# A two-layer conditional mixture-of-experts kernel on one core: LoRA sums, slot table and attention loop rearranged

## The reference, cut to what matters

```python
w = cond_weights[conditions]                     # layer 0: a 32x32 matrix for each batch
y = einsum('bct,bcd->bdt', x, w)
logits = y @ gate.T + 2 * y @ (gate_B @ gate_A).T
top 2 of 8 experts; gup = y @ gate_up + 2 * (y @ A.T) @ B.T   # LoRA of rank 16
out = silu(gates) * h @ down + 2 * LoRA          # 256 -> 128 -> 256
x = x + weighted sum of the two experts' rows
q, k, v = x @ Wq, Wk, Wv; rms norm, rope          # layer 1: 8 heads, 4 key groups, 32 wide
k_blocks[blk, :, off] = k; v_blocks[...] = v      # written over a cache of 4112 blocks of 16 rows
o = softmax(q k^T / 16, window of 128) v; o @ Wo
out = top 1 of 2 experts of width 1024, times its probability; x = x + out
```

## Time and profile before

| | |
|---|---|
| median of 3 runs | 1004.19 us (1002.6 to 1004.86) |
| profiled execution | 1012.61 us, span 1010.6 us, mean PE clock 0.905 |
| PE busy | 864.8 us, 86% of the span |
| DVE, POOL, ACT busy | 601.9, 432.6, 419.4 us |
| chain that ended last | PE 67%, DVE 13%, DMA 8%, issue 6% |
| HBM | 151.92 MB read, 41.75 MB written |

### The profile page before, as it was taken

The page is one execution under the profiler, slowest core; times in us unless marked ns, Lnnn a source line. Parts: engine busy times, 40 slices in busy tenths (PEclk is TensorE's granted clock), DMA queues, the critical chain, the costliest instruction groups (busy, mean ns, idle before and its releaser), DMA issues.

```text
span 1010.6 us, 28469 instructions
## 1 busy us (share of the span) xinstructions
PE 864.8 (86%) x9102; PEld 658.2 (65%) x9102; DVE 601.9 (60%) x2374; ACT 419.4 (42%) x1293; POOL 432.6 (43%) x454
## 2 busy tenths in 40 slices
PE   4778879999576766079999999999949999999996
PEld 2436758888332322047777777777739999999995
DVE  6518946777489999454778778787812222222221
ACT  2332113333143333043767767676713333333331
POOL 0105255554477772432455656556212233333332
PEclk9976789999799889555999999999968999999998
DMA  6973845556754441242455555555235565656561
GB/s 181 335 291 143 268 161 158 164 161 151 246 166 142 142 144 60 77 117 69 121 154 140 142 139 144 144 143 151 73 129 167 188 216 185 210 181 210 192 203 37
DMA packets 103850, 162.85 MB, mean 161 GB/s; under 512 B 29129, under 2 KB 83963, under 8 KB 98224
## 3 DMA queue, kind: packets, MB, share of 16 engines
q1 hardware_dynamic: 66768, 85.55, 26.3%
q0 software_dynamic: 32208, 68.36, 23.8%
q10 hardware_dynamic: 4800, 7.96, 2.5%
HBM read 151.92 MB, written 41.75 MB: 192 GB/s over the span
## 4 chain that ended last, share of the span: by engine, by line
PE 67%; DVE 13%; DMA 8%; issue 6%; POOL 2%; ACT 1%; DVEq 1%; SPq 0%; POOLq 0%; ACTq 0%
PE bank L958 12%; PE bank L969 11%; PE bank L930 8%; PE bank L942 7%; PE bank L831 6%; PE bank L910 6%; DMA work<-in_x 4%; PE bank L918 4%; PE bank L895 3%; PE bank L823 3%; DVE work L1162 2%; DVE work L1341 2%; POOL work L478 2%; DVE work L1338 2%; PE bank L839 2%
## 5 line engine op out<-in xcount | busy, mean ns | idle before, releaser
L1430 DVE TENSOR_TENSOR work<-bank,work 128x512 f32<-128x512 f32 x66 | 45.7, 692 | 166.9 <-ACT work L708 166.9
L958 PE MATMUL bank<-work,experts 128*128 128x128 f32 x1056 | 130.9, 278 | 0.5 <-ACT work L700 0.5
L958 PEld LDWEIGHTS bank<-work,experts 128*128 128x128 f32 x1056 | 127.9, 195 | 2.5 <-ACT work L700 0.9
L969 PE MATMUL bank<-experts,work 128*128 x528 | 124.6, 379 | 0.0
L691 ACT ACTIVATE work<-work 128x164 f32<-128x164 f32 x256 | 107.7, 425 | 22.1 <-DVE work L1418 21.9
L478 POOL DMA_INDIRECT kvring<-in_cache,read_i x64 | 65.2, 1018 | 100.8 <-PE bank L942 35.6
L677 ACT ACTIVATE wqkv_sb<-bank 105x512 f32<-105x512 f32 x128 | 75.8, 592 | 75.1 <-PE bank L930 74.2
L482 POOL DMA_INDIRECT out_x<-work x33 | 33.5, 1017 | 164.5 <-DVE work L1442 158.9
L969 PEld LDWEIGHTS bank<-experts,work 128*128 128x128 f32 x528 | 95.4, 190 | 10.3
L478 POOL DMA_INDIRECT work<-y_rows,index_work x72 | 67.8, 942 | 70.1 <-PE bank L839 46.8
L855 PE MATMUL bank<-wqkv_sb,work 128*128 128x512 f32 x128 | 73.4, 702 | 21.1 <-DVE work L1329 21.1
(11 more groups left out here) (244 smaller groups left out, 1596.9 us busy)
## 6 DMA issues: line engine op xcount, KB each, us to landing
experts<-in_fc SPq DMA_DIRECT2D x33, 1024.0 KB, 5.2
work<-cst SPq DMA_DIRECT2D x128, 82.0 KB
slots_out<-work SPq DMA_DIRECT2D x72, 128.0 KB, 2.3
work<-in_x SPq DMA_DIRECT2D x64, 128.0 KB, 3.1
written_blocks<-kvring POOLq DMA_DIRECT2D x3, 2048.0 KB, 7.6
slots_in<-fill ACTq DMA_DIRECT2D x1, 4257.0 KB, 21.9
work<-slots_in SPq DMA_DIRECT2D x33, 129.0 KB, 5.1
y_rows<-rows SPq DMA_DIRECT2D x8, 512.0 KB, 6.1
```

Source lines behind the costliest of these rows:

```text
L958: mm = pe.matmul(bank[1 + n][:, k * P:k * P + P], fc_s[tile % 2][:, h * H1 + n * 512 + k * P:h * H1 + n * 512 + k * P + P], yst[tile % 2][ ...
L969: mm = pe.matmul(bank[5 + tile % 2][:, 0:D], av[n][:, k * P:k * P + P], proj_v[:, (4 * n + k) * D:][:, bass.ds(expert, D)], start=(n == 0 ...
```

## The change

Stage 1: two of the four block-diagonal DMAs go from SP to ACT. The LoRA factors are loaded by eight DMAs of POOL at the start, even experts to partitions 0 to 15 and odd ones to 64 to 79. The expert weights are loaded in two halves by ACT at tiles 5 and 10. The LoRA products move from after the last tile into the loop over tiles (PE at steps 13 to 27, two experts side by side), and DVE adds them to the weights. The block copies start after 26 tiles. `match_blocks` and `owners` move into stage 2 as index steps 3 to 23, all later index steps move back by 10 or 20. `hi_hot` becomes one DVE instruction for a chunk, and ACT multiplies by the token's number in eight. The slot buffer is filled by 17 DMAs in stage 2.

Stage 3 and 4: the ring has 12 places (four in the room of the gate-up weights), and its first 12 `cached` gathers are started within stage 3, one for every second tile from tile 4. The attention goes by couples: at each step PE does the first batch's values of couple s-3, the key transposes of couple s+2, the ranks at every fourth step, both batches' transposed probabilities of couple s-2 (two PSUM banks), the output product at every second step, the second batch's values of couple s-3 and both batches' scores of couple s+1 (one pair of banks for a couple).

```diff
-RING = 8
+RING = 12
@@ sync, scalar: block-diagonal DMAs
-            for j in range(BT):
+            for j in range(2):
                 sp.dma_start(bd[...], cw_dram...).then_inc(s1_bd, 16)
+            for j in range(2, BT):
+                act.dma_start(bd[...], cw_dram...).then_inc(s1_bd, 16)
@@ gpsimd, stage 1
+            for j in range(2):
+                place = lora[64 * j:64 * j + R0, :].rearrange("r (k c) -> r k c", c=896)
+                for a, c0, width in ((gup_a, 0, 256), (gup_bt, 256, 256), (down_a, 512, 128), (down_bt, 640, 256)):
+                    pool.dma_start(place[:, :, c0:c0 + width], ...).then_inc(s_lora, 16)
-            pool.wait_ge(s1_yc, 12)
+            pool.wait_ge(s1_yc, 26)
             stage_blocks(0)
             copy_blocks(0)
             pool.wait_ge(s_stw, 16)
             stage_blocks(1)
-            for e in range(E0):
-                pool.wait_ge(s_foldc, 2 * e + 2)
-                pool.tensor_tensor(gup_v[...], product[e % 4][:, 0:512], gup_v[...], ALU.add)
-                pool.tensor_tensor(down_v[...], product[e % 4][:, 512:768], down_v[...], ALU.add)
-                if e == 3:
-                    copy_blocks(1)
+            copy_blocks(1)
             pool.wait_ge(s_stw, 32)
             stage_blocks(2)
@@ gpsimd, stages 3 and 4
+                if i == 4:
+                    pool.wait_ge(s_idx, 1)
+                if i >= 4 and i % 2 == 0 and i // 2 - 2 < RING:
+                    cached(i // 2 - 2)
...
-            for i in range(RING):
-                cached(i)
...
-            for s in range(B + 20):
-                i = s // 2 - 3 + RING
-                if s % 2 == 0 and RING <= i < B // 2:
-                    cached(i)
-                if s % 2 == 1 and RING <= i - 1 < B // 2:
-                    wait(pool, s4_pv, min(s - 4, B))
-                    written(i - 1)
+            for s in range(4, NC + 11):
+                if s - 4 + RING < NC:
+                    cached(s - 4 + RING)
+                if RING <= s - 5 + RING < NC:
+                    pool.wait_ge(s4_kt, s + 2)
+                    written(s - 5 + RING)
@@ scalar
-                if st.s == 6:
-                    act.dma_start(gup_v[:, 0:2048], gup[:, 0:2048]).then_inc(s_exp0, 16)
-                if st.s == 12:
-                    act.dma_start(gup_v[:, 2048:4096], gup[:, 2048:4096]).then_inc(s_exp0, 16)
-                if st.s == 18:
-                    act.dma_start(down_v, down).then_inc(s_exp0, 16)
+                if st.s == 5:
+                    act.dma_start(gup_v[:, 0:2048], gup[:, 0:2048]).then_inc(s_exp0[0], 16)
+                    act.dma_start(down_v[:, 0:1024], down[:, 0:1024]).then_inc(s_exp0[0], 16)
+                if st.s == 10:
+                    act.dma_start(gup_v[:, 2048:4096], gup[:, 2048:4096]).then_inc(s_exp0[1], 16)
+                    act.dma_start(down_v[:, 1024:2048], down[:, 1024:2048]).then_inc(s_exp0[1], 16)
+            for chunk in range(8):
+                act.wait_ge(s_oht, chunk + 1)
+                for k in range(8):
+                    n = chunk * 8 + k
+                    ins = act.activation(hi_tok[chunk % 4][:, k * N0:k * N0 + N0], hi_hot[chunk % 4][:, k * N0:k * N0 + N0],
+                                         ACT.Copy, scale=c("tokid")[:, n % NT:n % NT + 1])
+                ins.then_inc(s_ohs, 1)
@@ tensor, stage 1 (PE)
+                if st.s in range(13, 13 + 2 * E0, 4):
+                    k = (st.s - 13) // 4
+                    wait(pe, s_folded, 4 * k)
+                    for h in range(2):
+                        for j in range(2):
+                            part = lora[64 * j:64 * j + R0, k * 896:k * 896 + 896]
+                            mm = pe.matmul(bank[6 + j][:, h * 256:h * 256 + 256], part[:, h * P:h * P + P], part[:, 256:512], ...)
+                if st.s in range(15, 15 + 2 * E0, 4):
+                    ...   # the same for the down weights, one matmul for each j
@@ tensor, stage 4: order of one step (couple s)
+                values(st, False)            # couple s-3, first batch
+                # key transposes of couple s+2; group_ranks at every fourth step
+                # for both batches of couple s-2: 4 transposes to tbank[q]
+                # output product at every second step
+                values(st, True)             # couple s-3, second batch
+                # for both batches of couple s+1: 4 score matmuls
@@ vector
-                for k in range(8):
-                    ins = dve.tensor_scalar(hi_hot[:, n * N0:n * N0 + N0], c("slotno")[:, 0:N0], hi_f[:, n:n + 1],
-                                            c("tokid")[:, n % NT:n % NT + 1], ALU.is_equal, ALU.mult)
+                dve.tensor_tensor(hi_hot[chunk % 4].rearrange("p (n s) -> p n s", n=8),
+                                  hi_f[:, chunk * 8:chunk * 8 + 8, None].broadcast_to([P, 8, N0]),
+                                  c("slotno")[:, None, 0:N0].broadcast_to([P, 8, N0]), ALU.is_equal).then_inc(s_oht, 1)
+            def fold(n):
+                k, dst, width = n // 2, (gup_v, down_v)[n % 2], (512, 256)[n % 2]
+                dve.wait_ge(s_exp0[k // 2], 32)
+                dve.wait_ge(s_fold, n + 1)
+                for j in range(2):
+                    e = 2 * k + j
+                    dve.scalar_tensor_tensor(out=dst[...], in0=bank[6 + j][:, 0:width], scalar=2.0,
+                                             in1=dst[...], op0=ALU.mult, op1=ALU.add).then_inc(s_folded, 1)
+                elif 3 <= s < 3 + NE + NR:      # match_blocks, one a step
+                elif 17 <= s < 24:              # owners, two a step
```

More of the change, by code:

```diff
@@ L671, in _, with exponentials @@
             stage3_drained(act)
-            for st in skewed(act, B, 8, 5, 12):
-                if st.has(-3):
-                    q = st.slot(-3) % 2
-                    act.wait_ge(s4_tp, st.s - 2)
-                    wait(act, s4_pv, st.s - 4)
-                    act.activation(pt[q], tbank[0:KP, :], ACT.Copy).then_inc(s4_tpc, 1)
-                if st.q % 4 == 3 and st.has(-7):
-                    tile, t = 2 * st.turn(-7) + st.slot(-7) // 4, st.slot(-7) // 4
+            def exponentials(st, q):
+                k = 2 * (st.slot() % 2) + q
+                act.wait_ge(s4_ttr, 4 * st.s + 2 * q + 2)
+                if q == 0:
+                    wait(act, s4_pn, st.s - 1)
+                for g in range(2):
+                    act.activation(pr[k][:, g * NK:g * NK + NK], sc[k][:, g * NK:g * NK + NK], ACT.Exp,
+                                   bias=mn[k // 2][:, 2 * q + g:2 * q + g + 1], scale=-1.0,
+                                   accum_out=sm[k // 2][:, 2 * q + g:2 * q + g + 1]).then_inc(s4_ex, 1)
@@ L684, in _ @@
                     act.wait_ge(s4_w, tile + 1)
                     act.activation(col(rows, tile * RW, D), vbank[t][:, D:2 * D], ACT.Copy).then_inc(s4_wc, 1)
[L686 to L692 removed]
+                if st.has(0):
+                    exponentials(st, 0)
@@ L695, in _ @@
+                if st.has(-2):
+                    x = st.slot(-2) % 2
+                    wait(act, s4_pv, 2 * st.s - 6)
+                    for n, q in enumerate((x, 1 - x)):
+                        act.wait_ge(s4_tp, 2 * st.s - 3 + n)
+                        act.activation(pt[2 * x + q], tbank[q][0:KP, :], ACT.Copy).then_inc(s4_tpc, 1)
+                if st.has(0):
+                    exponentials(st, 1)
             for st in skewed(act, 2 * N1, 8, 3, 2):
@@ L776, in _ @@
             pe.matmul(bank[7][:, 0:NT * E0], c("ones"), onehot0, start=True, stop=True).then_inc(s_rank, 1)
-            for e in range(2, E0):
-                fold(e)
             pe.wait_ge(s_cmp, 1)
@@ L807, in _ @@
             pe.wait_ge(s_te0, 1)
-            pe.wait_ge(s_folded, 2 * E0)
             def expert_of(te, tile, n):
@@ new lines, in _ @@
+            for st in skewed(pe, NC, 12, 2, 12):
+                if st.has(-3):
+                    if not st.has(0):
+                        pe.wait_ge(s4_tpc, 2 * st.s - 5)
+                    if not st.has(0) and st.slot(-3) % 2 == 0:
+                        pe.wait_ge(s4_wc, (st.s - 3) // 2 - 1)
+                    values(st, False)
+                if st.has(2):
+                    q = st.slot(2)
+                    pe.wait_ge(s4_in[q], 32 * st.turn(2) + 32)
+                    wait(pe, s4_ktc, st.s + 2)
@@ L914, in _ @@
-                if st.q % 4 == 0 and st.has(-8):
-                    tile, t = 4 * st.turn(-8) + st.slot(-8) // 4, st.slot(-8) // 4 % 2
+                if st.q % 4 == 3 and st.has(-11):
+                    group_ranks(3 * st.turn(-11) + st.slot(-11) // 4)
+                if st.has(-2):
+                    x = st.slot(-2) % 2
+                    pe.wait_ge(s4_pn, st.s - 1)
+                    for n, q in enumerate((x, 1 - x)):
+                        wait(pe, s4_tpc, 2 * st.s - (4 if n == 0 else 5))
+                        if n == 1 and st.has(-3):
```

(7 more changed lines are left out.)

359 lines of the change are left out of this document (166 added, 193 removed).

## The result

The changed kernel takes 977.19 us, the median of four runs (974.61 to 981.06); the kernel before took 1004.53 on the same chip (1002.6 to 1006.79). The ratio is 0.9731, 95% interval 0.9698 to 0.9763: 27 us faster, within the range (936 to 980) and near its upper end, 20 us above the forecast of 957 and outside the 948 to 968 that were thought likeliest. That holds for the chip of this result and the first of the experiments. On four other chips, met later, the kernel before takes 1095 to 1104 us and the changed one, measured on one of them, 1191.17: 1.079 times the median of before's seven runs there. The record's ratio for it, 1.096 (interval 1.075 to 1.117), counts only the two fastest of the seven.

What follows compares the result with a forecast made beforehand. PE bounds the kernel, busy 864.8 of 1010.6 us, so gains come where it waits or runs at half clock. Terms -20 + 1.8 + 3 - 10.4 - 21 from 1012.6 give 966.0, median 957; range 936 to 980.

Steps and rivals of the forecast that it cites:

- (b): POOL becomes stage 3's bound, +9; block chain or serial LoRA pairs hold stage 1, +5 each: 974 us, chance 0.16.
- (c): DVE or handshakes pace the attention at 4.4 us a couple as before, 19 us more: 976 us, chance 0.09.
- the step from one execution to the median: Whole kernel: the median lies 8.4 us below the profiled execution, so 966.0 becomes 957.6, rounded to 957.
- Stage 1, 16.3 for 20: Up to the first y gather: 20 us gained, bounds 12 and 27.
- The three terms: Stage 1 gains: stream of x to the last logits 3.1 us, steps to the one-hots 4.8, slot table 12.1.
- the second term: Stage 1, last logits to one-hots: 4.8 us gained, as top_two no longer delays logits and POOL's sums no longer run beside DVE.
- Stage 2, 7.1 for 1.8: Stage 2 costs 1.8 us, from seven reductions at 1.88 us a tile; matches and fill DMAs cost nothing.
- Stage 3, 8.9 for 3, bound 12: The 12 added gathers on POOL cost stage 3 3 us, at its start, bounds 0 and 12.
- Attention, 28.7 for 21, inside 8 to 35: Attention takes 286 us against 306.9, couples at 4.10 us, 30 us at half clock: gain 21, bounds 8 and 35.
- Rival (a): The clock comes back early in the attention, within 10 us, and x streams freely in stage 1: 940 us, chance 0.17.
- Rival (d): The clock falls in the attention, a couple at half clock costing 3.1 us more: 1044 us, chance 0.05.
- What would show it: Signs: first y gather near 110 us, DVE's gather wait under 3, couples 4.1 apart; against: attention clock between 0.5 and 1.

Runs made afterwards that it cites:

- Run 4: The kernel before with only the change's stage 1 and 2 part, stage 3 and attention as before: 994.54 us, ratio 0.9883.
- run 1: The changed kernel with one fill DMA ahead of stage 2's loop in place of 17 inside it: 978.48 us, ratio 0.9748.
- run 7: The changed kernel with PE's attention loop written out, cached gathers late and the fill in stage 3: 1174.02 us on the second chip (before 1095.63).
- run 2: The changed kernel with PE's attention loop written out instead of a loop of 12 couples: 960.93 us, ratio 0.955.
- 11: The changed kernel again, unaltered, on the fourth chip: 1191.17 us, 1.079 times the median of the kernel before.
- 12: The kernel before, unaltered, run for its trace on the fifth chip: 1095.01 us, ratio 1.0023 to itself.
- 10: The kernel of run 7, unaltered, on the third chip: 1182.12 us, ratio 1.076.
- 6: The changed kernel with PE's attention loop written out and the cached gathers late: 1183.89 us on the second chip, ratio 1.079.

## Why the prediction was right, and where its terms were off

**The mechanism.** Faster by three savings (stage 1, the cached gathers, the attention), in the stages where they were put; each of the first five lines of the table has the sign that was forecast. The sizes are another matter: the number fell within the range because errors of both signs met, and it lies beside rivals (b) and (c), 974 and 976, not in the forecast's own 948 to 968. The forecast for the profiled execution was 966.0 and it took 974.6: 8.6 us, the sum of +3.7 in stage 1, +5.3 in stage 2, +5.9 in stage 3, -7.7 in the attention and +1.5 in the rest. The other 11.0 of the 20 us come from the step from one execution to the median. I took off the 8.4 by which before's profiled execution stood above its median; after's stands 2.6 below its own. Run 4 suggests where the 8.4 lay: its old attention has 15 us less of half clock and is 7.6 us shorter. So the attention's saving of 28.7 is flattered by the one execution, and 21.1 is nearer to what the medians saw.

**Stage 1, 16.3 for 20.** The three terms were 3.1, 4.8 and 12.1; the trace has 1.9, 3.3 and 11.0. The stream itself is 3.7 us shorter (57.3 for 61.0, forecast 59.1), but the first product comes at 19.4, not at 16.5, after 2.0 us of waiting for x. That PE's start would gain from SP's two freed issues was wrong. PE's products wait 5.4 us for x in all (before 11.7, forecast 8), all of it before 40. The LoRA products take PE 7.3 us for 6.4; the 0.43 us that I took for one of L733's compares a matmul with a tile's two, and 24.2 us / 64 is 0.38. In the second term `top_two` still stands in front of the last logits, for which PE waits 1.91 us (before 1.58), so that half of its reason failed; the DVE instructions that POOL's sums had stretched are short again. In before's first two chunks of the slot table it was L1162 that was held (6.18 and 3.23 us for 1.82), with one tile as input, and not L1157, with two (1.23 and 1.13 for 1.13). The slot table was right within 1.1; the new bound is ScalarE at 2.0 us a chunk where I had DVE at 1.82.

**Stage 2, 7.1 for 1.8.** The step that failed is "17 fill DMAs of ACT, 0.4 us each, lie in its free time". They do lie in ScalarE's free time, and still cost some 0.28 us a tile of four and a little at the stage's end: 2.7 and 1.8 us by run 1, 2.9 and 0.3 by run 7, so 3 to 4.5 in all. PE stands for some 0.2 us longer, with "issue", ahead of L849, where it reads the tile's expert. Whether it is that read, the gather or the fetch of instructions that the fill's transfer delays, no run tells. The seven reductions took about what was forecast: their seven steps 12.7 to 13.0 us for 11.4. Some 1 to 2 us of the stage's growth have no owner.

**Stage 3, 8.9 for 3, bound 12.** Rival (b) came true in this stage, below its price (9 above the 3; measured 5.9 above them, 7.3 by run 4): POOL issues without a pause up to 389, and the added gathers cost 10.3 us by run 4. The other half of the rival, stage 1 held by the block chain or the LoRA pairs, did not come true. I had weighed POOL's busy time and its lead of 10 us, and DVE indeed waits hardly longer for the gathered rows (6.8 us in stage 3 for 5.9). What counts is what stands behind each gather, a scatter whose landing frees the buffer that ScalarE waits for. The early gathers so paid for themselves and no more.

**Attention, 28.7 for 21, inside 8 to 35.** Two errors of opposite sign. The clock came back 15 us after the first key transposes, not 30, and without the gaps the attention takes 275.5 us, 44.2 less than in before's trace and 36.6 less than in run 4. The couples were right: 4.0 us in run 2 (4.10 forecast; rival (c) had 4.4). Rival (a) came half true: it had 10 us to the clock and no wait for x. Against that stand 15.5 us that no step had: PE's loop body grew from 8 couples to 12 and is fetched anew in each of its three jumps. The change to `skewed(pe, NC, 12, 2, 12)` was in the diff, and I counted its matmuls, not its instructions. That 21 and 21.1 (run 4's comparison) agree is luck: the gaps ate what the early clock gave.

**Rival (d),** the clock falling in the attention, did not decide here: the falls went with the gaps. On the other kind of chip the window from 480 to 870 stands at 0.69. Its 49 couples would need some 196 us of PE at 4.0 each; PE is busy for 307 and idle for 83. So by this estimate more of the loss is work at half clock than waiting, and which of the two brings the other is not separated.

**The sums.** 957.6 is 958 when rounded, and rival (b)'s 957 + 9 + 5 + 5 is 976, not 974. Neither changes the range.

**What would show it.** Right: the clock at 1.00 early, key transposes 4.2 us after the first `written`, 5.4 us of waiting for x, POOL without a gap to tile 26 and beyond, couples 4.0 apart where no gap falls, and eight transposes in 0.88 us of the chain (0.96 behind the ranks). Near: first `y` gather at 113.5 for 110; DVE's wait for the gathers 6.8 us, where under 3 was named and the kernel before had 5.9. Wrong: tiles of 1.9 us for seven tiles only; windows with a clock between 0.5 and 1, which I had named as a sign against me, and which came from the loop. That sign is one of the forecast's being wrong, and for the attention's path it was: a cost stood there that the forecast did not have.

The Trainium skill's rule that activity releases the clock ("TensorE: Matmul & The Clock Gate", Part 1, What's actually happening) fares better after than before. The window 440 to 470 shows PE busy throughout at 1.00, and each of the three gaps was followed by half clock. The 37 us at 0.50 of before stay against it, and so do run 4's 32 us.

## What to carry to other kernels

When an unrolled loop's body grows, look at its instructions as well as its work: here a body of 12 couples cost 3 us at each jump and the clock after it, one of 8 showed no such gap, and writing the loop out gave back 16 us (960.93, the fastest measured on the first kind of chip). Work moved in front of an in-order queue's scatter costs what waits for that scatter, however idle the mover looks. And measure a change of an engine's order on more than one chip: this one takes 2.7% off the time on one and adds 8% on another. And one profiled execution is not the median: an old stretch at half clock was 47 us long in one trace and 32 in another of the same code.

## What the runs showed of the hardware

On four of the five chips of the experiments, all met after the first batch, the kernel before takes 9% to 10% longer and the changed one 22%, all of it in stage 3 and the attention; each of the other stages takes the same time within 1.1 us in runs 11 and 12. There the couples of the changed kernel take some 8 us as long as POOL's gathers fill the ring and 3.3 to 5.0 as soon as they have ended. The traces of these chips hold a third fewer semaphore records (10,900 to 11,600 for some 16,900), so that many waits there have no releaser; why PE is held up while the ring's gathers run stays open.

A 258 KB fill DMA every fourth tile, issued by an engine with free time, slows a PE-bound loop by some 0.28 us at most of them; the same bytes in one DMA ahead of the loop cost the loop's first gathers 5 us, and moved to the next stage nothing that shows (stage 3 174.1 and 175.9 us for 174.6, runs 7, 10 and 6).
